# The end of an attention stage in another order, two stores sent earlier, and VectorE's small routing steps written with a scalar stage

## The reference, cut to what matters

```python
x = x + _msa(_layernorm(x, ln1_w, ln1_b), w_qkv, w_proj)
x = x + _moe_mlp(_layernorm(x, ln2_w, ln2_b), gate_w, gate_b, w1, w2)
# _msa: q, k, v of each batch; softmax(q k / sqrt(8)) v, then @ w_proj
# _moe_mlp, with xf the rows:
logits = xf @ gate_w + gate_b
one_hot = jax.nn.one_hot(jnp.argmax(logits, axis=-1), E, dtype=xf.dtype)
h = jax.nn.gelu(jnp.einsum('td,edh->teh', xf, w1), approximate=True)
y = jnp.einsum('teh,ehd->ted', h, w2)
out = jnp.einsum('te,ted->td', one_hot, y)
```

## Time and profile before

| what | us |
|---|---|
| median of 3 runs (614.55 to 619.65) | 617.62 |
| the profiled execution, its own time | 619.02 |
| its span, first to last instruction | 617.3 |
| attention and routing, within the span | about 394 to 527 |
| experts, within the span | about 527 to 617 |

### The profile page before, as it was taken

One profiled execution on the slowest core, in us unless ns is written; L12 is line 12 of the kernel. 1 busy time (PEld: TensorE's weight loads), 2 busy tenths in 40 slices (PEclk: granted clock), 3 DMA queues, 4 the chain that ended last, 5 costly groups with the idle time before them and its releaser, 6 DMA issues. The chain is left out here.

```text
span 617.3 us, 35472 instructions
## 1 busy us (share of the span) xinstructions
PE 504.6 (82%) x15374; PEld 414.1 (67%) x15374; DVE 363.5 (59%) x1161; ACT 283.4 (46%) x691; POOL 154.4 (25%) x258
## 2 busy tenths in 40 slices
PE   0888988888986979799999768689888861599995
PEld 0777887877874654566665568567666650499995
DVE  4655555555553257566666448458899977155552
ACT  5221212221212864355456335678667731377772
POOL 2111111111114600000000030143466637055553
PEclk9899999999997988999999989999899965599998
DMA  8060000000000007594230010000011103233330
GB/s 277 2 222 0 0 0 0 0 0 0 0 0 2 1 2 150 127 333 80 69 87 1 0 57 17 2 5 1 19 37 53 40 29 109 83 86 105 108 104 22
DMA packets 22655, 34.39 MB, mean 56 GB/s; under 512 B 3616, under 2 KB 15909, under 8 KB 22216
## 3 DMA queue, kind: packets, MB, share of 16 engines
q1 hardware_dynamic: 19824, 27.23, 16.0%
q0 software_dynamic: 2784, 6.56, 3.0%
HBM read 25.98 MB, written 8.26 MB: 55 GB/s over the span
## 5 line engine op out<-in xcount | busy, mean ns | idle before, releaser
L230 PE MATMUL ps_u<-v_cur,buf_b 128*32 128x32 f32 x7936 | 76.4, 198 | 6.3 <-DVE v_cur L287 1.4
L230 PEld LDWEIGHTS ps_u<-v_cur,buf_b 128*32 128x32 f32 x7936 | 72.7, 109 | 11.6 <-DVE v_cur L287 10.9
L215 PE MATMUL ps_v<-buf_a,u_pad 128*32 128x128 f32 x1984 | 62.9, 281 | 7.2 <-issue 5.8
L215 PEld LDWEIGHTS ps_v<-buf_a,u_pad 128*32 128x32 f32 x1984 | 54.3, 113 | 10.8 <-issue 9.1
L585 PE MATMUL ps_h<-buf_c,up 128*128 128x512 f32 x96 | 51.4, 642 | 0.4 <-DVE buf_c L777 0.4
L1700 POOL DMA_INDIRECT out<-yb,token_i x39 | 38.5, 986 | 49.7 <-DVE resid L1802 48.6
L195 ACT ACTIVATE over<-u_diff 128x32 f32<-128x32 f32 x31 | 7.1, 230 | 94.2 <-POOL u_diff L175 94.2
L179 POOL TENSOR_TENSOR u_hist<-inv_u,r_sum 128x16 f32 x62 | 13.7, 221 | 141.9 <-DVE inv_u L294 141.9
L1723 PE MATMUL m_h<-xT,w_near 128*128 128x128 f32 x312 | 43.1, 283 | 0.1
L1733 PE MATMUL m_y<-w,hid_t 128*128 x312 | 42.1, 279 | 0.1
L1276 POOL TENSOR_TENSOR vb<-vn,row_mask 128x1024 f32<-128x1024 f32 x16 | 30.3, 1892 | 44.8 <-ACT vn L1458 41.5
(11 more groups left out here) (305 smaller groups left out, 1132.8 us busy)
## 6 DMA issues: line engine op xcount, KB each, us to landing
cw_b<-cw_d SPq DMA_DIRECT2D x16, 512.0 KB, 7.7
xt<-sorted_x SPq DMA_DIRECT2D x39, 136.0 KB, 2.2
w<-in_w SPq DMA_DIRECT2D x2, 2048.0 KB, 16.9
buf_a<-in_x SPq DMA_DIRECT2D x4, 512.0 KB, 5.8
buf_b<-in_x_t SPq DMA_DIRECT2D x4, 512.0 KB, 7.0
buf_d<-in_x_nt SPq DMA_DIRECT2D x1, 2048.0 KB, 10.5
sorted_x<-nobody SPq DMA_DIRECT2D x1, 1088.0 KB, 4.8
out<-yb,token_i POOLq DMA_INDIRECT x39, 2.4
```

Of the source, the lines that this page charges most:

```text
L215: last = mm(ps_v[h][32 * j:32 * j + 32, 0:D], u_pad[:, h, j, 32 * i4:32 * i4 + 32], K[:, g * D:(g + 1) * D], start=i4 == 0, stop=i4 == TI - 1)
L230: last = mm(rows_u[h][32 * q:32 * q + 32, g, :], KT[:, b * N:(b + 1) * N], v_cur[:, h, k:k + 1].broadcast_to([P, WIDE]), start=True, stop= ...
```

## The change

Five edits, all in `attend_and_route`:

- GpSimd: behind the loop it waits for `o_mm` 15 (was 16), sends the two tiles that are left of the first 20, and only then waits for `o_mm` 16 and sends the other 12 (was: all 14).
- TensorE: behind the last body, the transposes of chunk 15 come first, then those of the output of chunk 14, then `rank`, then the mixing of chunk 15, and the output projection of chunk 14 behind it.
- ScalarE: `turned(15)` goes ahead of `output(14)` and the inverse root.
- VectorE, order: `scales` goes from behind `place` to behind `spread` in even chunks; from chunk 15 on the steps stand in a new order.
- VectorE, form: 11 `tensor_tensor` in `moments`, `scales` and `choose` become `scalar_tensor_tensor` with a multiplication of the first input by 1.0 ahead of the operation (`both`). Their counts and sizes stay.

```diff
+                pool.wait_ge(o_mm, NC - 1)
+                for t in range(sent, 2 * S.first[GROUPS - 3]):
+                    send(t)
                 pool.wait_ge(o_mm, NC)
-                for t in range(sent, G):
+                for t in range(2 * S.first[GROUPS - 3], G):
                     send(t)
...
                 body(NC - 1, 1, NC // 2 - 1)
+                turn(NC - 1, 1)
+                turn_output(NC - 2, 0)
                 pe.wait_ge(sub_done, NC)
                 rank(NC // 2)
-                turn_output(NC - 2, 0)
-                turn(NC - 1, 1)
+                mix(NC - 1, 1)
                 project_output(NC - 2, 0)
-                mix(NC - 1, 1)
...
+                turned(NC - 1)
                 output(NC - 2)
                 inverse_root(GROUPS - 2)
-                turned(NC - 1)
...
+                def both(out, a, b, op):
+                    return stt(out, a, 1.0, b, ALU.mult, op)
...
-                    c.step(tt(gap[:, gs], rstd[:, gs], rstd[:, gs], ALU.mult))
+                    c.step(both(gap[:, gs], rstd[:, gs], rstd[:, gs], ALU.mult))
...
-                for i in range(NC):
+                for i in range(NC - 1):
                     below_most(i)
                     if i >= 6 and i % 2 == 0:
                         place(i // 2 - 3)
-                    if i >= 4 and i % 2 == 0:
-                        scales(i // 2 - 2)
...
                     if i >= 2:
                         spread(i - 2)
+                    if i >= 4 and i % 2 == 0:
+                        scales(i // 2 - 2)
...
+                below_most(NC - 1)
+                add(NC - 3)
+                over_sum(NC - 2)
+                choose(GROUPS - 3)
+                spread(NC - 3)
+                moments(GROUPS - 2)
                 place(GROUPS - 3)
+                over_sum(NC - 1)
+                add(NC - 2)
                 scales(GROUPS - 2)
                 choose(GROUPS - 2)
-                add(NC - 2)
-                over_sum(NC - 1)
+                add(NC - 1)
+                place(GROUPS - 2)
                 spread(NC - 2)
-                add(NC - 1)
                 spread(NC - 1)
                 moments(GROUPS - 1)
-                place(GROUPS - 2)
                 scales(GROUPS - 1)
                 choose(GROUPS - 1)
                 place(GROUPS - 1)
```

More of the change, by code:

```diff
@@ L1551, in moments @@
                     dve.wait_ge(own, c.n)
-                    c.step(tt(gap[:, gs], six[:, gs, 1], six[:, gs, 4], ALU.subtract))
-                    tt(total[:, gs], six[:, gs, 1], six[:, gs, 4], ALU.add).then_inc(own, 1)
+                    c.step(both(gap[:, gs], six[:, gs, 1], six[:, gs, 4], ALU.subtract))
+                    both(total[:, gs], six[:, gs, 1], six[:, gs, 4], ALU.add).then_inc(own, 1)
                     c.n = c.n + 1
-                    c.step(tt(var[:, gs], six[:, gs, 2], six[:, gs, 5], ALU.add))
+                    c.step(both(var[:, gs], six[:, gs, 2], six[:, gs, 5], ALU.add))
                     c.step(stt(gap[:, gs], gap[:, gs], 0.25, gap[:, gs], ALU.mult, ALU.mult))
@@ L1561, in scales @@
                     dve.wait_ge(rooted, n + 1)
-                    c.step(tt(gap[:, gs], rstd[:, gs], rstd[:, gs], ALU.mult))
+                    c.step(both(gap[:, gs], rstd[:, gs], rstd[:, gs], ALU.mult))
                     c.step(stt(gap[:, gs], var[:, gs], LN_EPS, gap[:, gs], ALU.add, ALU.mult))
                     c.step(ts(gap[:, gs], gap[:, gs], -0.5, 1.5, ALU.mult, ALU.add))
-                    c.step(tt(rows[:, gs, ROOT], rstd[:, gs], gap[:, gs], ALU.mult))
+                    c.step(both(rows[:, gs, ROOT], rstd[:, gs], gap[:, gs], ALU.mult))
                     stt(rows[:, gs, SHIFT], total[:, gs], -0.5, rows[:, gs, ROOT], ALU.mult, ALU.mult).then_inc(row_ends, 1)
@@ L1572, in choose @@
                         dve.wait_ge(slots_done, IDLE + n + 1)
-                    c.step(tt(logits[:, gs, :], rows[:, gs, D:WIDE], rows[:, gs, ROOT:ROOT + 1].broadcast_to(wide), ALU.mult))
-                    c.step(tt(logits[:, gs, :], logits[:, gs, :], gate_bias[:, None, :].broadcast_to(wide), ALU.add))
+                    c.step(both(logits[:, gs, :], rows[:, gs, D:WIDE], rows[:, gs, ROOT:ROOT + 1].broadcast_to(wide), ALU.mult))
+                    c.step(both(logits[:, gs, :], logits[:, gs, :], gate_bias[:, None, :].broadcast_to(wide), ALU.add))
                     c.step(v.tensor_reduce(top[:, gs], logits[:, gs, :], AX.X, ALU.max))
-                    c.step(tt(eq[:, gs, :], logits[:, gs, :], top[:, gs, None].broadcast_to(wide), ALU.is_equal))
-                    c.step(tt(eq[:, gs, :], eq[:, gs, :], prefer[:, None, :].broadcast_to(wide), ALU.mult))
+                    c.step(both(eq[:, gs, :], logits[:, gs, :], top[:, gs, None].broadcast_to(wide), ALU.is_equal))
+                    c.step(both(eq[:, gs, :], eq[:, gs, :], prefer[:, None, :].broadcast_to(wide), ALU.mult))
                     c.step(v.tensor_reduce(top[:, gs], eq[:, gs, :], AX.X, ALU.max))
-                    tt(hot[:], eq[:, gs, :], top[:, gs, None].broadcast_to(wide), ALU.is_equal).then_inc(hot_done, 1)
+                    both(hot[:], eq[:, gs, :], top[:, gs, None].broadcast_to(wide), ALU.is_equal).then_inc(hot_done, 1)
                 def place(n):
```

## The result

The changed kernel takes 628.21 us (median of 6, 625.08 to 630.77), the kernel before 618.08 in the same comparison (median of 6, 614.55 to 621.54). The ratio is 1.0158, 95% interval 1.0111 to 1.0204: about 10 us slower, and 2.7 above the upper end of the predicted range. The profiled execution took 630.77 us, its span is 629.1 (617.3 before), the mean granted clock 0.932 (0.942).

A forecast was written before the change was run, and what follows sets the result against it. VectorE was taken to bound the loop, GpSimd the end. Loop +2.6, clock +2.7 and end -3.1 gave +2.2 us: 621.2 from the profiled 619.02, 619.8 against 617.62, called 620, range 610.5 to 625.5.

The forecast's parts named there:

- The stalls and who is caught: VectorE's loop: with scales last, GpSimd's vb catches choose in odd chunks; stalls 2.8 us a pair instead of 2.1.
- B: VectorE's loop: the new form escapes the stall beside vb, about 10.5 us, and the end's 3.1: 604 us; chance 0.08.
- D: Loop: choose isn't caught by vb; gains of five times 3.2 and the end's 3.1 give 611.3 us; chance 0.14.
- The loop without the clock, +2.6: Chunks 4 to 15, falls of the clock left out: late choose and rank make the loop 2.6 us longer.
- the ring: Steady loop: closed chain from rank through scores, projection, vb and choose to the next rank, 14.2 us against 13.60 a pair.
- two falls in the five pairs: TensorE's loop: 3.2 us stops before rank drop the clock twice in five pairs, 1.4 us each, +2.7 us.
- Rival C: TensorE's loop: the stop before rank drops the clock in every pair, five falls, +7.0, 624 us or more; chance 0.16.
- The end, -3.1: Behind most of chunk 15: earlier last mixing and two early stores end the last store 3.1 us sooner (2.1 to 4.4).

The follow-up runs named there:

- the filled run: The changed kernel with five useless multiplications on TensorE behind the mixing of odd chunks 3 to 13: 620.63 us, ratio 0.9972 against the kernel before.

## Why the prediction was wrong, point by point

- **The stalls and who is caught: right, but for two points.** The new form stands still like the old one. `choose` is caught in each odd chunk from 5 on, for 1.66 to 1.86 us, ended by vb; the first step of `scales` takes 0.89 to 0.98 where about 1.0 was expected; the wait before L1373 gave way to one before `rank`. Rivals B and D are out. What was wrong: steps with one input can be caught too (the conversion in `place`), and the steady loop of before had no stop ahead of the scores (L1337) that could have gone.
- **The loop without the clock, +2.6: about right, a little low.** With the stop filled, chunk 4 to 15 is 77.90 - 74.32 = 3.6 longer than before, at full clock, and the ring 14.0 to 14.1 for 14.2. The filling has a price of its own in there that no run shows apart.
- **The clock, "two falls in the five pairs": the step that failed.** I had worked out a stop of 3.2 us, longer than the 2.38 behind which the clock had fallen once, and still counted two falls of five. There are five: the stops are 3.31 and four times 2.86. And each costs more than 1.4. From `rank` to `values` it is 3.53 us at full clock (458.42 to 461.95 with vb held), and 4.98, 5.96, 6.15, 4.84 and 5.20 in the changed kernel: 1.3 to 2.6 each, 9.5 together, and the two dearest, 2.4 and 2.6, are those with the longer stretch of half clock behind them. The term should have been about +9 and stood at +2.7. I had taken 1.4 from one fall with only 2.1 us of work in it; here the same 3.53 us of work took up to 6.15. Rival C, priced at 624 with "more if a fall lasts longer", was the mechanism, and 0.16 was too little for it: for every pair its condition had been met in my own sum.
- **The end, -3.1: right in kind, -3.8 measured.** `o_mm` 16 came at 7.7 behind `most` of chunk 15 for 8.5, the last `place` at 530.13 - 511.65 = 18.5 for 19.7, the last four stores 0.8 behind it for 0.2.
- **The sum.** By its terms, forecast and then measured: loop +2.6 and +3.1, clock +2.7 and +9.0, end -3.1 and -3.8, together +2.2 and +8.3. The 9.0 is 78.11 - 71.16 = 6.95 for the first four falls (chunk 4 to 14, against the filled run) and 2.0 for the last (chunk 14 to 15 in 8.31 for the 6.3 worked out); the 3.1 is what they leave of the loop's 12.1.

One thing in the first paragraph of the prediction stays open: whether VectorE with its 2.1 us of stalls really set the pace of the kernel before. Two traces without the 1.6 us stall of `scales` have pairs of the same 13.5 to 13.6 us; only with `scales` last and vb held for `choose` was a pair shorter, 12.58.

## What to carry to other kernels

When a step stands still beside another engine's long instruction, its move can just move the collision: here it went from `scales` to `choose`, or from `scales` to the conversion in `place`. Ask which steps stand behind each place that it can fall on, and which engine waits for them: with the stall on `scales` or on `place` a pair took 13.6 us, with the same stall on `choose`, for whose result TensorE waits, 14.0 at full clock and 15.3 to 16.7 with the falls. Holding the long instruction back by one wait brought 1.0158 to 0.9897; putting the step back where it was brought it to 0.9943, and these two can't be told apart by their intervals.

A stop of TensorE has two prices: its length, and that of the clock behind it. The length alone doesn't tell whether the clock falls. In the traces of this case it fell behind each of eleven stops of 2.86 to 3.31 us, behind seven of seventeen of 2.31 to 2.39, and sometimes behind shorter ones, of 2.19 and 1.67 us among them. So a sum shouldn't take one observed fall, or one absence of a fall, as a limit. But once a stop is clearly longer than one behind which the clock has fallen, as 3.2 was than 2.38, count a fall each time, and price it by all the work that follows at half clock.

## What the runs showed of the hardware that I had not expected

A conversion of 4 elements a row from float32 to int32, one input, SBUF to SBUF, stands still beside a GpSimd TENSOR_TENSOR like a step with two inputs: 1.73 and 1.77 us against 0.17. The normalisation's statistics (0.47 to 0.48, with or without vb) don't. The Trainium skill's page "SBUF — State Buffer", section "Who interferes with whom", counts copies and casts among what can contend, when their operands meet the conditions of a mode that uses two ports, beside steps with two SBUF inputs. The trace agrees that a cast can be held up (1.73 us); whether this one ran in such a mode no run here shows.

A stop of TensorE can be filled with useless work at a profit: 2.43 us of multiplications in each odd chunk kept the clock at 1.00 from 396 to 500 us and took 6.95 us off ten chunks. And in the two traces in which TensorE hardly stopped a pair took 13.4 to 13.7 us, with three gaps of about 0.46 us inside its runs of small multiplications, while with a stop of 1.39 us it went round in 12.58.
